# A graph attention layer with a linear layer: s1 rows by DMA, an end by tiles, and two tiles' matmuls that take turns

## The reference, cut to what matters

```python
# x [4096,128], adj [4096,4096] of 0 and 1, in2 [4096,128], a1, a2 [128,1]
def gnn(input1, in2, adj, a1, a2):
    e = input1 @ a1 + (in2 @ a2).T            # s1 of the row + s2 of the column
    e = where(e > 0, e, 0.2 * e)
    att = softmax(where(adj > 0, e, -9e15), axis=1)
    att = att * sum(adj, axis=1, keepdims=True)
    att = 0.1 * att + 0.9 * adj
    return att @ in2
x = x + gnn(layernorm(x), in2, adj, a1, a2)
x = x + layernorm(x) @ weight.T + bias
```

## Time and profile before

| | |
|---|---|
| median of 3 runs | 394.11 us |
| the profiled execution, its own time | 394.79 us |
| its span | 393.0 us |
| TensorE matmuls busy | 367.2 us, 93% |
| TensorE weight loads busy | 319.4 us, 81% |
| VectorE busy | 311.6 us, 79% |
| ScalarE busy | 250.6 us, 64% |
| GpSimd busy | 128.2 us, 33% |
| adj loads | 33.56 MB, 44.1% of 16 DMA engines |
| granted TensorE clock, mean | 0.992 |

### The profile page before, as it was taken

How to read it: one execution, slowest core, us unless ns; L and a number is a source line. 1 busy time by engine, 2 the same in 40 slices (tenths; PEclk the granted TensorE clock), 3 DMA queues, 4 the chain that set the end, 5 groups by cost and what they waited for, 6 DMA issues and landing times.

```text
span 393.0 us, 8864 instructions
## 1 busy us (share of the span) xinstructions
PE 367.2 (93%) x3237; PEld 319.4 (81%) x3237; DVE 311.6 (79%) x790; ACT 250.6 (64%) x638; POOL 128.2 (33%) x255
## 2 busy tenths in 40 slices
PE   0398999999999999999999999999999999999991
PEld 0277888888888888888888888888888888888881
DVE  3989889989995977959596886959598695959873
ACT  2797998797685673919376491928558291946100
POOL 1697141516250605033150604215060412400101
PEclk9999999999999999999999999999999999999996
DMA  7999997566674572909265381917447000000000
GB/s 200 242 213 214 220 186 161 109 135 124 145 139 103 103 154 44 211 17 175 67 128 131 66 189 18 196 56 140 104 88 169 15 13 15 3 1 15 15 0 30
DMA packets 17357, 42.81 MB, mean 109 GB/s; under 512 B 1936, under 2 KB 8608, under 8 KB 17312
## 3 DMA queue, kind: packets, MB, share of 16 engines
q0 software_dynamic: 9216, 33.56, 44.1%
q1 hardware_dynamic: 8096, 8.67, 7.0%
HBM read 73.66 MB, written 2.11 MB: 193 GB/s over the span
## 4 chain that ended last, share of the span: by engine, by line
PE 89%; DMA 7%; POOL 2%; DVE 1%; issue 0%; SPq 0%; POOLq 0%; ACT 0%; DVEq 0%
PE acc_u L599 29%; PE acc_v L599 29%; PE acc_y L599 26%; DMA adj_all<-adj 5%; PE small L593 2%; PE small L579 2%; DMA x_pre<-x 1%; PE turned L568 1%; POOL adj_all L334 1%; POOL pre_rstd L344 0%; POOLq L43 0%; POOL post_rstd L377 0%; DVE pre_st L739 0%; SPq L274 0%; DVE late L842 0%
## 5 line engine op out<-in xcount | busy, mean ns | idle before, releaser
L449 ACT ACTIVATE steep<-s_bc,steep_s 128x256 bf16<-128x256 f32 x512 | 208.0, 497 | 11.6 <-DVE plus L757 9.9
L599 PE MATMUL acc_y<-weights_y,adj_all 128*128 128x258 f16 x1024 | 121.9, 275 | 3.1 <-DMA adj_all<-adj 2.1
L599 PE MATMUL acc_v<-weights_v,minus 128*128 128x258 f16 x1024 | 120.3, 273 | 0.0
L599 PE MATMUL acc_u<-weights_u,plus 128*128 128x258 f16 x1024 | 120.3, 273 | 0.0
L599 PEld LDWEIGHTS acc_y<-weights_y,adj_all 128*128 128x128 bf16 x1024 | 100.2, 98 | 19.7 <-DMA adj_all<-adj 2.0
L599 PEld LDWEIGHTS acc_u<-weights_u,plus 128*128 128x128 bf16 x1024 | 99.7, 97 | 14.7
L599 PEld LDWEIGHTS acc_v<-weights_v,minus 128*128 128x128 bf16 x1024 | 99.8, 98 | 14.4
L757 DVE TENSOR_TENSOR plus<-adj_all,steep 128x2048 bf16<-128x2048 bf16 x64 | 78.5, 1227 | 2.5 <-ACT steep L449 2.5
L760 DVE TENSOR_TENSOR minus<-adj_all,plus 128x2048 bf16<-128x2048 bf16 x64 | 78.4, 1226 | 2.2
L462 ACT ACTIVATE num<-acc_u,ac 128x129 f32<-128x129 f32 x32 | 11.5, 363 | 104.8 <-PE acc_u L599 104.8
L374 POOL TENSOR_SCALAR post_var<-post_mv 128x2 f32<-128x2 f32 x16 | 3.4, 215 | 161.9 <-DVE post_mv L821 161.9
(11 more groups left out here) (78 smaller groups left out, 250.4 us busy)
## 6 DMA issues: line engine op xcount, KB each, us to landing
adj_all<-adj POOLq DMA_DIRECT2D x64, 512.0 KB, 9.4
plus<-in SPq DMA_DIRECT2D x4, 512.0 KB, 7.1
x_pre<-x SPq DMA_DIRECT2D x16, 128.0 KB, 6.2
x_res<-x SPq DMA_DIRECT2D x16, 128.0 KB, 6.3
out<-late SPq DMA_DIRECT2D x16, 128.0 KB, 1.7
s_rows<-s_bc SPq DMA_DIRECT2D x16, 1.0 KB
steep<-a SPq DMA_DIRECT2D x1, 64.0 KB, 3.4
a_bc<-a SPq DMA_DIRECT2D x1, 64.0 KB, 5.5
```

The lines of the kernel that those rows point to most:

```text
L449: ins = nc.scalar.activation(steep[:, h, k, :], s1_bc[b][:, :], ACT.Relu, bias=steep_s2[:, jt:jt + 1], scale=STEEP)
L599: ins = nc.tensor.matmul(acc[:, 0:2 * WC], left[:, jt, cols(t)], right[:, jt, :, :].rearrange("p a b -> p (a b)"), start=(jt == 0), stop=( ...
```

## The change

Three things are changed.

s1 by DMA: for chunks from `SPREAD` = 5 on there is no `spread` and no `copy_spread`. SyncE stores the 256 values of `pre_s1` straight to `s1_rows` once GpSimd has made them, waits until they are stored, waits until the sign tests of two chunks before are done, and loads the row into all partitions of `s1_bc`. ScalarE's sign tests wait for that load.

Turns: in slots 2 to 14 TensorE does U of both tiles, alternating tile by tile at each column tile, then `turn(c - 1)`, then V of both tiles in the same way, Y of both tiles for chunk c + 2, and `linear(c - 1)`. U waits for `tile_left` 2c, both epilogues of the chunk before. VectorE's order becomes masks 0, 1, 2, both epilogues, masks 3; ScalarE's sign tests 0, 1, both numerators, sign tests 2, the copies, sign tests 3. Slot 1 keeps its order. Y reads 257 columns instead of 258.

End by tiles: slot 15 goes tile by tile, with `linear(14)` ahead of V of tile 1 and a transpose of tile 0 ahead of its last quarter. Moments, normalisation, transpose, copy, linear layer, output and store of chunk 15 are done for each tile on its own. The range check goes to slots 10 to 13, a quarter in each.

```diff
+SPREAD = 5
+        def s1_in(n, b):
+            return 16 * ((n - b) // 2 - (SPREAD - b + 1) // 2 + 1)
...
             def store_s1(n, b):
-                sp.wait_ge(s1_ready, n + 1)
-                sp.dma_start(s1_rows[n:n + 1, :], s1_bc[b][0:1, :]).then_inc(s1_stored[b], 16)
+                if n < SPREAD:
+                    sp.wait_ge(s1_ready, n + 1)
+                    sp.dma_start(s1_rows[n:n + 1, :], s1_bc[b][0:1, :]).then_inc(s1_stored[b], 16)
+                else:
+                    sp.wait_ge(pre_pool, PRE * n + 3)
+                    sp.dma_start(s1_rows[n].rearrange("(t p) -> p t", p=P), pre_s1[b][:, :],
+                                 allow_slow_non_contiguous=True).then_inc(s1_stored[b], 16)
+                    sp.wait_ge(s1_stored[b], landed(n, b))
+                    sp.wait_ge(steep_done, 4 * n - 4)
+                    sp.dma_start(s1_bc[b][:, :], s1_rows[n].partition_broadcast(P)).then_inc(s1_landed[b], 16)
...
-            post(CHUNKS - 1, (CHUNKS - 1) % 2)
+            last_rstd(last, 0)
+            pool.wait_ge(out_ready, last)
+            last_bias(last, 0, last % 2)
+            last_bias(last, 1, last % 2)
+            last_rstd(last, 1)
...
-                    [0, 1, "first", 2, 3, "second", "copies"]
+                    [0, 1, "first", "second", 2, "copies", 3] if ahead(c, 1) else \
+                    ["first", "copies", "second"]
...
+            def pair(acc, left, right, q, width=2 * WC):
+                ends = [None] * TILES
+                for jt in range(q * QJ, (q + 1) * QJ):
+                    for t in range(TILES):
+                        ends[t] = nc.tensor.matmul(acc[t][:, 0:width], left[:, jt, cols(t)], ...)
+                return ends
...
+                if not ahead(c, 1):
+                    pe.wait_ge(tile_left, 2 * c - 1)
+                    product(acc_u[0], plus[b], w_u, 0, plus_ready, c).then_inc(u_done, 1)
+                    product(acc_v[0], minus[b], w_v, 0, minus_ready, c).then_inc(tile_done, 1)
+                    turn(c - 1)
+                    pe.wait_ge(tile_left, 2 * c)
+                    product(acc_u[1], plus[b], w_u, 1, plus_ready, c).then_inc(u_done, 1)
+                    linear(c - 1)
+                    for q in range(QUARTERS - 1):
+                        quarter(acc_v[1], minus[b], w_v, 1, q)
+                    turn_tile(0)
+                    quarter(acc_v[1], minus[b], w_v, 1, QUARTERS - 1).then_inc(tile_done, 1)
+                    return
...
-                    for t in range(TILES):
-                        pe.wait_ge(tile_left, 2 * c + t - 1)
-                        product(acc_u[t], plus[b], w_u, t, plus_ready, c).then_inc(u_done, 1)
-                        if t == 1:
-                            if ahead(c, 2):
-                                spread(c + 2, b)
-                            turn(c - 1)
-                        product(acc_v[t], minus[b], w_v, t, minus_ready, c).then_inc(tile_done, 1)
+                    pe.wait_ge(tile_left, 2 * c)
+                    masked_pair(acc_u, plus[b], w_u, plus_ready, u_done, c)
+                    if c + 2 < SPREAD:
+                        spread(c + 2, b)
+                    turn(c - 1)
+                    masked_pair(acc_v, minus[b], w_v, minus_ready, tile_done, c)
+                    if ahead(c, 2):
+                        y_pair(c + 2, (f + 2) % BUFS)
+                    linear(c - 1)
+                    return
...
-            turn(CHUNKS - 1)
-            linear(CHUNKS - 1)
+            linear_tile(0)
+            turn_tile(1)
+            linear_tile(1)
...
+                if c >= RANGE_AT - QUARTERS and c < RANGE_AT:
+                    range_check(c - RANGE_AT + QUARTERS)
+                if not ahead(c, 1):
+                    epilogue(c, 0, b)
+                    last_moments(c, 0)
+                    last_normal(c, 0, b)
+                    finish(c - 1, 1 - b)
+                    epilogue(c, 1, b)
+                    last_moments(c, 1)
+                    last_finish(c, 0, b)
+                    last_normal(c, 1, b)
+                    last_finish(c, 1, b)
+                    return
...
-                    [0, 1, "first", 2, 3, "second"]
+                    [0, 1, "first", 2, 3, "second"] if c == 1 else \
+                    [0, 1, 2, "first", "second", 3]
```

More of the change, by code:

```diff
@@ L165, in gnn_ffn @@
         s1_ready = sem("s1_ready")
+        s1_landed = [sem(f"s1_landed{b}") for b in range(2)]
         consts_ready = sem("consts_ready")
@@ L551, in _ @@
             run_slots(slot)
-            copy_turned(CHUNKS - 1)
+            for t in range(TILES):
+                act.wait_ge(xn_turned, CHUNKS + t)
+                if t == 0:
+                    act.wait_ge(ffn_done, CHUNKS - 1)
+                nc.scalar.activation(xn_t[:, cols(t)], xnt_ps[:, cols(t)], ACT.Copy).then_inc(xnt_ready, 1)
             with act.If(range_left(act) != 0):
@@ L595, in linear, with quarter @@
                 ins.then_inc(ffn_done, 1)
-            def quarter(acc, left, right, t, q):
+            def quarter(acc, left, right, t, q, width=2 * WC):
                 for jt in range(q * QJ, (q + 1) * QJ):
-                    ins = nc.tensor.matmul(acc[:, 0:2 * WC], left[:, jt, cols(t)],
-                                           right[:, jt, :, :].rearrange("p a b -> p (a b)"),
+                    ins = nc.tensor.matmul(acc[:, 0:width], left[:, jt, cols(t)],
+                                           right[:, jt, :, :].rearrange("p a b -> p (a b)")[:, 0:width],
                                            start=(jt == 0), stop=(jt == JT - 1))
@@ L609, in product, with masked_pair, y_pair @@
                 return ins
+            def pair(acc, left, right, q, width=2 * WC):
+                ends = [None] * TILES
+                for jt in range(q * QJ, (q + 1) * QJ):
+                    for t in range(TILES):
+                        ends[t] = nc.tensor.matmul(acc[t][:, 0:width], left[:, jt, cols(t)],
+                                                   right[:, jt, :, :].rearrange("p a b -> p (a b)")[:, 0:width],
+                                                   start=(jt == 0), stop=(jt == JT - 1))
+                return ends
+            def masked_pair(acc, left, right, ready, signal, c):
+                for q in range(QUARTERS):
+                    pe.wait_ge(ready, 4 * c + q + 1)
+                    ends = pair(acc, left, right, q)
+                for ins in ends:
+                    ins.then_inc(signal, 1)
+            def y_pair(n, f):
+                pe.wait_ge(y_left, 2 * n)
+                for q in range(QUARTERS):
+                    pe.wait_ge(adj_landed[f][q], adj_in(n, f))
+                    ends = pair(acc_y, adj_b[f], w_y, q, WC + D)
+                for ins in ends:
+                    ins.then_inc(y_done, 1)
             pe.wait_ge(consts_ready, 1)
@@ L982, in slot, with last_moments, last_normal, last_finish @@
                 post_start(c)
-                if not ahead(c, 1):
-                    finish(c - 1, 1 - b)
+            def last_moments(n, t):
+                if t == 0:
+                    wait_apart(dve, post_pool, 2 * n)
+                wait_apart(dve, tile_left, 2 * n + t + 1)
+                nc.vector.bn_aggr(post_mv[:, t, :], post_st[:, t, :]).then_inc(post_moments, 1)
+            def last_normal(n, t, b):
+                dve.wait_ge(post_pool, 2 * n + 2 * t + 2)
+                dve.wait_ge(post_moments, 2 * n + t + 1)
+                if t == 0:
+                    dve.wait_ge(xn_turned, n)
+                nc.vector.tensor_scalar(xn[:, t, :], x1[b][:, t, :], post_mv[:, t, 0:1],
+                                        post_rstd[:, t:t + 1], ALU.subtract, ALU.mult).then_inc(xn_ready, 1)
+            def last_finish(n, t, b):
+                dve.wait_ge(ffn_done, n + t + 1)
+                dve.wait_ge(x1b_ready, n + t + 1)
+                if t == 0:
+                    dve.wait_ge(out_stored[b], 16 * (n // 2))
+                nc.vector.tensor_tensor(o_buf[b][:, cols(t)], ffn_ps[:, cols(t)], x1_bias[:, t, :],
+                                        ALU.add).then_inc(out_ready, 1)
             run_slots(slot)
-            last = CHUNKS - 1
-            post_end(last, last % 2)
-            finish(last, last % 2)
             with dve.If(range_left(dve) != 0):
```

49 lines of the change are left out of this document (36 added, 13 removed).

## The result

The changed kernel takes 395.55 us (median of 20 runs, 394.33 to 398.95), the kernel before 394.05 in the same comparison. The ratio is 1.004, 95% interval 1.0024 to 1.0057: slower by 0.4%, clear of no change. Forecast were 394.7, that is 0.6 us more than before, less than the 0.8 us that the forecast itself called the least that can be told from no change; of the three signs it gave slower the largest chance, 0.42.

What follows compares the result with a forecast made beforehand. TensorE's unbroken run of matmuls was taken to bound the kernel from 35 us on. Terms -4.9 - 0.3 + 0 + 4.2 + 3.15 - 1.5 = +0.6 us on the median 394.11 gave 394.7, range 392.4 to 397.2.

Steps and rivals of the forecast that it cites:

- 1, s1 spreads off TensorE: Slots 3 to 13 drop four small matmuls each, with s1 arriving by DMA at no cost: -4.9 us.
- 2, Y one column narrower: Y's 64 matmuls in each of 12 slots take less time at 257 columns than at 258: -0.3 us.
- 3, turns: 2432 matmuls change accumulator at each step, at no cost: 0, bounds -2.4 to +2.4 us.
- 4, slot 2 waits: Paired U of chunk 2 waits for both epilogues of chunk 1, leaving TensorE idle: +4.2 us, bounds 3.9 to 4.4.
- rival (a): TensorE's clock falls in the wait of slot 2, costing +2.2 us: time 396.9; chance 0.28.
- 5, slots 14 and 15: U of chunk 15 waits for the first epilogue, then late masks; other work precedes V's end: +3.15 us, bounds 2 to 4.
- 6, the end: After the last V, finishing chunk 15 tile by tile shortens the tail: -1.5 us, bounds -1.0 to -2.3.
- rival (b): A matmul that changes accumulator is cheaper by 1.0 ns, 2432 times: -2.4 us, time 392.3; chance 0.10.
- signs of being wrong: Slot 2 gap well under 4 us, matmul pitch other than 111.7 ns, or gaps in the middle slots.
- Rival (d): The s1 row's store and load take over 22 us, delaying 11 slots; 1 us late makes 405; chance 0.05.

Runs made afterwards that it cites:

- turns alone: The kernel before with only the turns in slots 2 to 14 and their VectorE and ScalarE orders; 400.16 us, ratio 1.0159.
- two and two: The changed kernel with two matmuls of tile 0, then two of tile 1, neighbours sharing no moving columns; 396.95 us, ratio 1.0065 to the kernel before.

## Why the prediction was right, and where it wasn't

In the order of its terms, in us, by the two profiled executions. The forecast of 394.7 came within 0.9 us of the median, but in part by luck: two steps were wrong in opposite directions and nearly cancel, as the table shows.

| step | forecast | measured | by |
|---|---|---|---|
| 1, s1 spreads off TensorE | -4.9 | -4.9 | 11 x 0.447; no wait of TensorE on s1 |
| 2, Y one column narrower | -0.3 | 0 | 3.58 us for 32 with 257 as with 258 |
| 3, turns | 0 | -2.4 | 2432 x 1.0 ns |
| 4, slot 2 waits | +4.2 | +4.2 | 4.23 idle ahead of U |
| clock, left to rival (a) | 0 | +1.8 | U 8.89 against 7.08 |
| 5, slots 14 and 15 | +3.15 | +3.4 | U of chunk 14 to the end of the last V: 32.84 against 29.57, and 0.13 that the turns save there |
| 6, the end | -1.5 | -1.3 | -2.0 to the last add, +0.7 behind it |
| start-up, not in the forecast | 0 | -0.4 | TensorE's chain begins at 34.57, before at 35.01 |
| sum | +0.6 | +0.4 | spans 393.0 and 393.3 |

The two losses that decide the sign, the wait of slot 2 and those of slot 15, were read rightly from the timelines: where they stand, who releases them and how long they are. Mended, they came back: the ratio fell from 1.004 to 0.981, 9.1 us. The waits (4.2, 1.7, 0.8) and the clock (1.8) make 8.5 of these, less 0.1 for the turns that slot 14 gives up; 0.7 us stay open.

Two steps failed. **Term 3** took 0 within bounds of 2.4 either way, and the truth lies on a bound. The start-up rows couldn't tell it: 24 changes of 1 ns in 192 matmuls are 0.02 us in 21.45, the rounding of the rows. I took "not seen" for "not there" and gave rival (b) 0.10; turns alone show it happened in full. By the forecast's own signs of being wrong, a pitch other than 111.7 ns is one: it was 110.8, and the slots were 21.92 us instead of 22.1.

**The clock** was left out of the likeliest case, at 0.28. The row of the end had the fall after 3.95 us of idling, and the wait of slot 2 was to be about 4.0: that was close to the same thing, and the forecast should have had it in the sum. It couldn't be certain: at the end of the changed kernel TensorE idles 3.77 us ahead of the transpose, and the granted clock in that profile is 1.00 from 384 to 388.3. So part of term 6 is luck too: in the profile with the wait filled, with the clock at 0.68 and 0.50 there, the transpose and the products take 0.4 us more. The price of 2.2 us was read from the start-up, whose row shows a granted clock of 1.00 and so doesn't show that those matmuls were slow by the clock; measured were 1.8.

The rule of the Trainium skill, page "TensorE: Matmul & The Clock Gate", section "HAM oscillation — how this bites in real kernels", that a gap between bursts puts the clock to half, holds here with 0.50 after a wait of 4.2 us, though not after each such wait. Section "A second HAM failure mode: psum-queue depth-cycling" of the same page of the Trainium skill tells of a kernel that cycles through PSUM banks and idles briefly between its groups of matmuls, and whose clock falls again and again. Here the banks change at each matmul without any idling, and the granted clock is 1.00 from 109.85 to 131.77 us and from 120 to 340: the change of bank alone doesn't bring the clock down, and the turns were faster than no turns.

**Term 2** was 0.3 for nothing: the step "time goes with columns" has no support in any run here.

**The s1 row** is right in its cost and wrong in its size. 17 us into the slot was forecast; 22.9 came in the slot shown, just past the 22.8 up to which I had it free at all, and 26.2 in the latest, at the very edge of the about 26 us up to which I had it free. The store of 256 values took 9.4 us on average, the upper bound, and 13.4 at longest. The reckoning of the slack was right: after the latest row the second epilogue ended 0.25 us before U started, so nothing was lost, and hardly anything was left. Rival (d) had far less distance than its chance of 0.05 says.

That the median moved by 1.5 us and the profile by 0.4 has two parts. The profiled execution of the kernel before was 0.7 above its median, which is scatter. That of the changed kernel was 0.4 below, and there the low clock has a share: its length differs between executions, the mean granted clock of the 20 lies between 0.979 and 0.991, and the profiled one has 0.991. The five executions with 0.990 or 0.991 take 395.1 us on average, the nine with 0.982 or 0.983 take 396.1. So in a typical execution the clock costs up to about 1 us more than the 1.8 of the table, as U's 9.62 us in the profile of two and two shows too.

## What to carry to other kernels

When an order is made to wait for all of a group instead of a part of it, look at the first and the last round, where the neighbours have another order: the waits here, 4.2 us in slot 2 and 1.7 and 0.8 us at chunk 15, sit there and none in the eleven rounds between. A wait of 4 us on TensorE can cost more than itself (4.2 us of wait and 1.6 to 2.5 of low clock here); fill it or mend it first. And try turns between two accumulators, with neighbours that take different column tiles: 110.2 ns instead of 111.8 at the same instruction count, 2304 times here. And when a transfer's slack is reckoned, set it against the latest one: the s1 row came 22.9 us into its slot in the one shown first, and 26.2 at the latest.

## What the runs showed of the hardware that was not expected

- The pace of 128x258 matmuls depends on the order: 111.8 ns on one accumulator, 111.4 changing at every second, 110.8 at each, 110.2 at each with other moving columns. Whether the last 0.6 ns come from the moving columns or from the weights, which change places with them, is open, and so is why the accumulator matters.
- 257 columns take as long as 258: 3.58 us for 32 matmuls without turns, 7.09 for 64 with them.
- A store of 256 single 4-byte values, 1 KB in all, takes 8.0 to 13.9 us beside the adj loads until the next issue of its queue, and lets the 512 KB adj loads take 14.9 us instead of 9.4 (median), at 60.6% instead of 44.1% of the DMA engines. In this kernel TensorE waits for none of them.
- A wait of about 4 us on TensorE doesn't bring the same fall of the clock each time. In the profiles with slot 2's wait it fell in the wait (two and two), as U began, or 1 us after that (turns alone); after 3.77 us at the end of the changed kernel it hadn't fallen.
- The last store split in two halves: 3.9 us from the last add to the end of the span instead of 3.2, so the split end gives back a third of what it gains. The other profiles agree, with 3.5 to 4.1 us with the new end and 3.0 to 3.4 with the old; no run has the split store alone.
